# Reordered scorer, first exponents and last batch in a fused gating, mixture and masked-pooling kernel

## The chip, the cores and the metric

One core of a Trainium2 chip. The metric is the device time of one execution in microseconds (us); lower is better. The output is [8, 512, 256] in float32.

## The reference

Eight batches of 512 tokens with 256 features. Two layers add to x.

```
u  = zX * lap_x(x) + zY * lap_y(x) + zR * x * (1 - x)
w  = softmax over the top 2 of (u @ router)             # 8 experts
x  = x + sum_e w_e * (act(u @ gate_up_e + b_e) @ down_e + b'_e)
score = tanh(x @ W1 + b1) @ v                           # per token
mask(j, l) = l <= j | l >= j | l != j                   # by the batch's kind 0, 1, 2
pooled = softmax_l(score, masked) @ x / count(mask row)
x  = x + fp8(pooled / s_in) @ fp8(kernel / s_k) * (s_in * s_k) + bias
```

The fp8 rounding is done with float32 operations on a grid; everything else is float32, with products in two or three parts (hi and lo) where a plain one would lose digits.

## The kernel before, in words

The engines run programs of their own, in strict program order, and meet at semaphores. SP issues the loads and stores, GpSimd (POOL) the indirect and the accumulating transfers. PE is TensorE, ACT ScalarE, DVE VectorE. There are four stages: the differences and the routing (to about 130 us), 71 blocks of 128 gathered rows through their expert (to about 348 us), mixing and scoring (to 403 us), and the pooling with the fp8 layer. The change touches the last two.

**Mixing and scoring**, n = 0 to 7. DVE adds the two weighted expert rows of batch n to X (`mix_of`, semaphore `mixed`), and makes X_lo of the batch before (`x_low`, once X_hi is there). ACT's `scores_of(n)` copies X_hi(n), then the two halves of the transposed batch from PSUM (xT), then does the tanh of the batch before (`hide(n-1)`). PE does `x_transposed(n)`, `hide(n-1)` (the scorer's product with W1) and `score(n-2)` (the product with v), then at the end hide(7), score(6), score(7). hide(n) waits for both xT(n), score(n) for tanh(n).

**Statistics.** The 4096 scores stand in score_col [128, 32]; PE transposes them, and DVE makes running maxima over each row from the left and from the right, from them the row maxima for the three kinds of mask (`row_max`), the maximum of each row (own_max, spread by a product), `gap` and `reach`. ACT copies or exponentiates them in parts: decay, four diagonals of decay_lhs, reach_lhs, max_rhs, in that order. Four low parts follow on DVE, and then POOL multiplies max_rhs with the spread matrix once for each batch, `spread_gaps(n)`, all eight in a row. PE's `exponents(n)` begins with the product of score_lhs and gaps_rhs(n).

**Pooling**, a software pipeline over n = 0 to 9. PE: sums_of(n), feed_forward(n-2), pool_of(n), quant_transposed(n-1), exponents(n+2). ACT: exponents(n+1), ffn_out(n-2), pool_out(n) (pooled, then scaled), turned_quant(n-1). DVE: rounding(n-1) (two operations on grid, lift, quant), norms(n), lows(n+1) (probs_lo, falls, states), add_bias(n-2). POOL: `add_up(n)` waits for ffn_sum(n) and for the store of X(n), and adds ffn_sum to the output in memory with an accumulating transfer. ffn_sum has two buffers: add_bias(n) waits until add_up(n-2) has landed. SP stores X(n) as soon as batch n is mixed.

Of the kernel before, what the change touches and what calls it, by code (L numbers as in the profile page):

```python
# [25 lines left out]
ALU = mybir.AluOpType  # L26
ACT = mybir.ActivationFunctionType
# [53 lines left out]
def adaln_ffn_kernel(nc, x, zx, zy, zr, kinds, router_w, gate_up_w, gate_up_b, down_w, down_b,  # L81
# [7 lines left out]
    TB = S // P  # L89
    NT = B * TB  # L90
# [22 lines left out]
    with ExitStack() as ctx:  # L113
        def sem(name):
            return ctx.enter_context(nc.semaphore(name))
# [127 lines left out]
        from_left = sb("from_left", [P, P])  # L243
        from_right = sb("from_right", [P, P])
# [118 lines left out]
        hi_set = sem("hi_set")  # L363
# [28 lines left out]
        begun = [sem(f"begun{i}") for i in range(B)]  # L392
# [29 lines left out]
        def _(sp):  # L422
# [54 lines left out]
            for n in range(B):  # L477
                sp.wait_ge(mixed, n + 1)
                sp.dma_start(out_v[n], X[:, n * TB:(n + 1) * TB, 0:H]).then_inc(begun[n], 16)

        @block.gpsimd
        def _(pool):
# [101 lines left out]
            def add_up(n):  # L584
                pool.wait_ge(ffn_sum_ready, n + 1)
                pool.wait_ge(begun[n], 16)
                pool.dma_start(out_v[n], ffn_sum[:, n % 2], accum_op=ALU.add).then_inc(result_stored[n % 2], 16)  # L587

            pool.wait_ge(lo_set, 4)
            for n in range(B):  # L590
                spread_gaps(n)
            for n in range(B):
                add_up(n)
            for s in range(2):
                pool.wait_ge(result_stored[s], 16 * (B // 2))

        @block.scalar
        def _(a):
# [127 lines left out]
            a.activation(score_lhs[0:2 * R], bank[0][0:2 * R, 0:P], ACT.Copy).then_inc(hi_set, 1)  # L726
            a.wait_ge(gap_col_ready, 1)
            a.activation(decay[:], gap[:], ACT.Exp).then_inc(hi_set, 1)
            for q in range(QS):
                op = a.activation(diagonal(q), gap[:], ACT.Exp)  # L730
            op.then_inc(hi_set, 1)
            a.wait_ge(reach_ready, 1)
            a.activation(reach_lhs[0:2 * R], reach[0:2 * R].unsqueeze(1).broadcast_to([2 * R, QS, R]),
                         ACT.Copy).then_inc(hi_set, 1)
            a.wait_ge(max_ready, 1)
            a.activation(max_rhs[2 * R:P], row_max[2 * R:P], ACT.Copy).then_inc(hi_set, 1)
# [38 lines left out]

            exponents(0)
            for n in range(B + 2):
                if n + 1 < B:
                    exponents(n + 1)
                if n >= 2:  # L780
                    ffn_out(n - 2)
                if n < B:
                    pool_out(n)
                if 1 <= n <= B:
                    turned_quant(n - 1)

        @block.tensor
        def _(pe):
# [174 lines left out]
            def exponents(n, kind):  # L963
                pe.wait_ge(spread_ready, n + 1)
                wait_count(pe, probs_ready, n)
                pe.matmul(bank[0][:], score_lhs[:], gaps_rhs[:, n].rearrange("p t n -> p (t n)"), start=True, stop=False)
                pe.matmul(bank[0][:].rearrange("p (t n) -> p t n", n=P), ident_b[:],
                          masks[:, ds(kind), :].broadcast_to([P, TB, P]), start=False, stop=True).then_inc(gaps_psum, 1)
                wait_count(pe, fall_ready, n)
                pe.matmul(bank[1][:], reach_lhs[:].rearrange("p q r -> p (q r)"),  # L970
                          gaps_rhs[:, n].rearrange("p t n -> p (t n)"), start=True, stop=True).then_inc(falls_psum, 1)
                wait_count(pe, states_lo_ready, n)
                for t in range(TB):
# [57 lines left out]
            pe.wait_ge(lo_set, 4)  # L1031
            pe.wait_ge(tables, DECAY_CLEAR)
            exponents(0, kind_of(0))
            exponents(1, kind_of(1))
            for n in range(B + 2):
                if n < B:
                    sums_of(n)
                if n >= 2:
                    feed_forward(n - 2)
                if n < B:  # L1040
                    pool_of(n)
                if 1 <= n <= B:
                    quant_transposed(n - 1)
                if n + 2 < B:
                    exponents(n + 2, kind_of(n + 2))

        @block.vector
        def _(dve):
# [309 lines left out]
            dve.memset(max_rhs[0:R * 2].bitcast(F32), 1.0)  # L1358
            def x_low(n):
# [12 lines left out]
            def stat(instruction):  # L1372
# [5 lines left out]
            LOWEST = -3.0e38  # L1378
            dve.tensor_tensor_scan(from_left[:], score_row[:], score_row[:], LOWEST, ALU.max, ALU.max)
            stat(dve.tensor_tensor_scan(from_right[:, ::-1], score_row[:, ::-1], score_row[:, ::-1], LOWEST,  # L1380
                                        ALU.max, ALU.max))
            dve.tensor_scalar(own_max[:], ident[:, 0:R], from_left[:, P - 1:P], None, ALU.mult).then_inc(own_max_ready, 1)
            dve.tensor_tensor(around[:, 1:P - 1], from_left[:, 0:P - 2], from_right[:, 2:P], ALU.max)
            dve.tensor_copy(around[:, 0:1], from_right[:, 1:2])
            dve.tensor_copy(around[:, P - 1:P], from_left[:, P - 2:P - 1])
            stat(dve.tensor_scalar(row_max[:], from_left[:], kind_col[:, PREFIX:PREFIX + 1], None, ALU.add))
            stat(dve.scalar_tensor_tensor(out=row_max[:], in0=from_right[:], scalar=kind_col[:, POSTFIX:POSTFIX + 1],
# [4 lines left out]
            dve.tensor_tensor(gap[:], score_col[:, 0], max_bank, ALU.subtract).then_inc(gap_col_ready, 1)  # L1392
# [4 lines left out]
            dve.wait_ge(hi_set, 5)  # L1397
            dve.wait_ge(max_ready, 1)
            dve.tensor_tensor(score_lhs[R:2 * R], score_row[R:2 * R], score_lhs[R:2 * R].bitcast(F32),
                              ALU.subtract).then_inc(lo_set, 1)  # L1400
            dve.tensor_tensor(reach_lhs[R:2 * R], reach[R:2 * R].unsqueeze(1).broadcast_to([R, QS, R]),
                              reach_lhs[R:2 * R].bitcast(F32), ALU.subtract).then_inc(lo_set, 1)
            dve.tensor_tensor(max_rhs[3 * R:P], row_max[3 * R:P], max_rhs[3 * R:P].bitcast(F32),
                              ALU.subtract).then_inc(lo_set, 1)
# [47 lines left out]

            lows(0)
            for n in range(B + 2):
                if 1 <= n <= B:
                    rounding(n - 1)
                if n < B:
                    norms(n)
                if n + 1 < B:
                    lows(n + 1)  # L1460
                if n >= 2:
                    add_bias(n - 2)

# [22 lines left out]
```

## Time and profile before

| what | us |
|---|---|
| median of 3 runs | 501.81 (499.57 to 503.17) |
| the profiled execution | 498.88 |
| its span, first to last instruction | 496.9 |
| busy in the span: PE, DVE, POOL, ACT | 380.9, 368.8, 252.0, 221.3 |
| mean granted TensorE clock | 0.855 |

The profile is of one execution. Its span is shorter than its time by what lies around it. Busy time is a sum over the span; which engine sets the pace differs from stage to stage and is read from stretches of the trace. PEclk is the granted clock of TensorE as a share of full speed.

### The profile page before, as it was taken

Reading aid. Unit: us, or ns where it says so; the run is one execution under the profiler, and the core shown is the slowest. Engines: PE = TensorE matmul, PEld = TensorE weight load, DVE = VectorE, ACT = ScalarE, POOL = GpSimd, SP = SyncE. Lnnn points to the kernel's source line nnn. Section 1 sums busy time; section 2 is a strip of 40 time slices with the busy share of each in tenths; the row PEclk is TensorE's granted clock in tenths of the full one; section 3 lists DMA queues with packets and bytes.
Section 4 is the critical chain, followed back from the end, with each engine's and each line's share of the span. In section 5 each row is a group of like instructions: output and inputs, shape, how many; then the busy total and the mean of one; then the engine's idle time right before and its main releaser. Section 6 shows DMA issues by size and latency. Waiting matters only on the chain.

```text
span 496.9 us, 7816 instructions
## 1 busy us (share of the span) xinstructions
PE 380.9 (77%) x2269; PEld 325.7 (66%) x2269; DVE 368.8 (74%) x877; ACT 221.3 (45%) x480; POOL 252.0 (51%) x236
## 2 busy tenths in 40 slices
PE   0768886514299999999999999998188949887740
PEld 0657775513188888888888888887144538786630
DVE  7897777599667777888878877785499553778740
ACT  3473433100034444444444544443165545799850
POOL 6997564036557677777766666753300051021221
PEclk9976669655589999999999999999579966899975
DMA  6465651100033222322322322230699200034444
GB/s 215 142 212 174 191 174 48 39 0 1 21 95 97 86 87 77 106 87 91 94 90 83 97 86 69 92 86 26 206 350 368 92 0 1 1 54 76 63 71 78
DMA packets 39544, 50.02 MB, mean 101 GB/s; under 512 B 6126, under 2 KB 33138, under 8 KB 39506
## 3 DMA queue, kind: packets, MB, share of 16 engines
q0 software_dynamic: 11040, 21.90, 17.3%
q1 hardware_dynamic: 24242, 23.43, 14.9%
q10 hardware_dynamic: 4224, 4.19, 2.6%
q8 instruction: 22, 0.36, 0.3%
q14 instruction: 16, 0.13, 0.1%
HBM read 28.49 MB, written 21.89 MB: 101 GB/s over the span
## 4 chain that ended last, share of the span: by engine, by line
PE 55%; DVE 18%; issue 12%; POOL 6%; ACT 4%; DMA 2%; SPq 1%; DVEq 0%; POOLq 0%; ACTq 0%
PE bank L865 30%; PE bank L862 5%; PE bank L826 4%; PE bank L856 3%; PE bank L881 3%; DVE lift L1441 2%; DVE flow L1192 2%; ACT scaled L761 2%; DVE pair L1188 2%; POOL x_lo L515 2%; POOL pair L518 2%; DVE flow L1097 2%; PE bank L1000 2%; DVE gu_lo L1101 2%; PE bank L805 1%
## 5 line engine op out<-in xcount | busy, mean ns | idle before, releaser
L567 POOL DMA_INDIRECT y_rows<-outs,slot_dst x71 | 71.9, 1013 | 50.5 <-issue 29.9
L547 POOL DMA_INDIRECT rows<-u_rows,slot_src x71 | 71.8, 1012 | 24.8 <-issue 19.8
L672 ACT ACTIVATE tanh<-gate 128x256 f32<-128x256 f32 x71 | 29.6, 417 | 99.8 <-DVE gate L1240 99.8
L865 PE MATMUL bank<-gu_hi,rowT_lo 128*128 x142 | 57.1, 402 | 0.0
L865 PE MATMUL bank<-gu_hi,rowT_hi 128*128 x142 | 56.6, 399 | 0.0
L865 PE MATMUL bank<-gu_lo,rowT_hi 128*128 x142 | 56.4, 397 | 0.0
L1240 DVE TENSOR_SCALAR gate<-bank 128x256 f32<-128x256 f32 x71 | 30.2, 425 | 23.9 <-PE bank L865 23.7
L657 ACT ACTIVATE rowT_hi<-bank 128x256 fp32r<-128x256 f32 x71 | 27.0, 380 | 40.0 <-PE bank L856 40.0
L587 POOL DMA_DIRECT2D out<-ffn_sum x8 | 12.2, 1528 | 63.4 <-DVE ffn_sum L1450 63.4
L1258 DVE TENSOR_TENSOR actT_lo<-bank,actT_hi 128x256 fp32r<-128x256 f32 x71 | 30.1, 425 | 15.5 <-ACT actT_hi L677 15.1
L865 PE MATMUL bank<-dn_lo,actT_hi 128*128 x142 | 40.2, 283 | 0.0
L865 PE MATMUL bank<-dn_hi,actT_hi 128*128 x142 | 40.0, 282 | 0.0
L865 PE MATMUL bank<-dn_hi,actT_lo 128*128 x142 | 39.9, 281 | 0.0
L826 PE MATMUL bank<-router_sb,uT 128*128 128x8 f32 x128 | 23.2, 318 | 16.2 <-DVE logits L1110 14.7
L826 PEld LDWEIGHTS bank<-router_sb,uT 128*128 128x128 f32 x128 | 22.5, 273 | 18.2 <-DVE logits L1110 16.1
L862 PE MATMUL bank<-gu_bias,ones 128*128 x71 | 34.3, 482 | 0.0
L580 POOL TENSOR_TENSOR gaps_rhs<-max_rhs,spread 128x512 fp32r<-128x512 f32 x8 | 8.9, 1147 | 48.0 <-DVE decay_lhs L1405 48.0
L1224 DVE TENSOR_TENSOR rowT_lo<-bank,rowT_hi 128x256 fp32r<-128x256 f32 x71 | 29.5, 415 | 4.6 <-ACT rowT_hi L657 4.6
L677 ACT ACTIVATE actT_hi<-bank 128x256 fp32r<-128x256 f32 x71 | 27.5, 387 | 11.2 <-PE bank L881 11.2
L856 PE MATMUL bank<-ident,rows 128*128 128x128 f32 x142 | 27.9, 279 | 5.8 <-DMA rows<-u_rows,slot_src 5.8
L1245 DVE TENSOR_TENSOR glu<-gate,up 128x256 f32<-128x256 f32 x71 | 30.4, 428 | 2.4
L865 PEld LDWEIGHTS bank<-gu_lo,rowT_hi 128*128 128x128 f32 x142 | 27.0, 190 | 6.6
(267 smaller groups left out, 1139.9 us busy)
## 6 DMA issues: line engine op xcount, KB each, us to landing
picks<-y_rows SPq DMA_DIRECT2D x16, 512.0 KB, 8.0
X<-in_x SPq DMA_DIRECT2D x8, 512.0 KB, 5.4
raw_gu<-in_L_ffn_gate_up_proj SPq DMA_DIRECT2D x8, 512.0 KB, 4.1
u_rows<-flow ACTq DMA_DIRECT2D x8, 512.0 KB, 2.9
out<-X SPq DMA_DIRECT2D x8, 512.0 KB, 7.6
out<-ffn_sum POOLq DMA_DIRECT2D x8, 512.0 KB, 5.8
raw_dn<-in_L_ffn_down_proj SPq DMA_DIRECT2D x8, 256.0 KB, 4.9
rows<-u_rows,slot_src POOLq DMA_INDIRECT x71, 2.8
```

The source lines that it names most:

```text
L547: pool.indirect_dma_start(out=rows[:, s, :], out_offset=None, in_=u_rows, in_offset=bass.IndirectOffsetOnAxis(ap=slot_src[:, n:n + 1], axi ...
L567: pool.indirect_dma_start(out=y_rows, out_offset=bass.IndirectOffsetOnAxis(ap=slot_dst[:, m:m + 1], axis=0), in_=outs[:, m % UNROLL, :], i ...
L672: a.activation(tanh[:, s % 2], gate[:, s % 2], ACT.Tanh, scale=ALPHA).then_inc(tanh_ready, 1)
L677: a.activation(actT_hi[:, s % 2], bank[4 + s % 2][:, 0:KI * P].rearrange("p (k n) -> p k n", k=KI), ACT.Copy).then_inc(actT_hi_ready, 1)
L826: mm = pe.matmul(logit_bank[:, t, :], uT[:, half, t * P:(t + 1) * P], router_sb[:, half, :], start=(half == 0), stop=(half == KH - 1))
L856: mm = pe.transpose(bank[2 + s % 2][:, half * P:(half + 1) * P], rows[:, s, half * P:(half + 1) * P], ident[:])
L862: pe.matmul(acc, ones2[:], bias, start=True, stop=False)
L865: mm = pe.matmul(acc, left[:, part, :], right[:, ds(expert), part, :].rearrange("p e f -> p (e f)"), start=False, stop=(part == parts - 1 ...
L1224: dve.tensor_tensor(rowT_lo[:, d], bank[2 + d][:, 0:KH * P].rearrange("p (k n) -> p k n", k=KH), rowT_hi[:, d].bitcast(F32), ALU.subtract) ...
L1240: dve.tensor_scalar(gate[:, d], bank[d][:, 0:I], LIMIT, 0.5, ALU.min, ALU.mult).then_inc(gate_ready, 1)
L1245: dve.tensor_tensor(glu[:, d], gate[:, d], up[:, d], ALU.mult).then_inc(glu_ready, 1)
L1258: dve.tensor_tensor(actT_lo[:, d], bank[4 + d][:, 0:KI * P].rearrange("p (k n) -> p k n", k=KI), actT_hi[:, d].bitcast(F32), ALU.subtract) ...
```

## The change

In the mixing, PE does hide(n-1), x_transposed(n), score(n-1), and ACT copies xT(n) before X_hi(n). In the statistics from_left and from_right get a border column, so that one operation makes `around`; gap is computed behind row_max; ACT copies max_rhs first, then reach_lhs, then decay and the diagonals; DVE makes the low parts one by one as they come and multiplies gaps_rhs of batch 0 itself; PE waits for each part where it uses it. POOL makes gaps_rhs of batches 1 to 7, each behind a probs_lo two batches back, then the accumulating stores of batches 0 to 6. Batch 7 is done in halves of 256 tokens from scaled to the output: DVE adds ffn_sum to X in SBUF, and SP stores each half plainly. The pipeline's loops end one batch earlier, and norms(7) comes before rounding(6).

```
@@ SP
-            for n in range(B):
+            for n in range(LAST_B):
                 sp.wait_ge(mixed, n + 1)
-                sp.dma_start(out_v[n], X[:, n * TB:(n + 1) * TB, 0:H]).then_inc(begun[n], 16)
+                sp.dma_start(out_v[n], X[:, n * TB:(n + 1) * TB, 0:H]).then_inc(begun, 16)
+
+            for h in range(2):
+                own = slice(h * HALF, (h + 1) * HALF)
+                sp.wait_ge(half_result, h + 1)
+                sp.dma_start(out_v[LAST_B][:, own], X[:, LAST_B * TB:(LAST_B + 1) * TB, 0:H][:, own]).then_inc(half_stored, 16)
+            sp.wait_ge(half_stored, 32)
@@ POOL
             def add_up(n):
                 pool.wait_ge(ffn_sum_ready, n + 1)
-                pool.wait_ge(begun[n], 16)
+                pool.wait_ge(begun, 16 * LAST_B)
                 pool.dma_start(out_v[n], ffn_sum[:, n % 2], accum_op=ALU.add).then_inc(result_stored[n % 2], 16)
-            pool.wait_ge(lo_set, 4)
-            for n in range(B):
+            pool.wait_ge(first_spread, 1)
+            for n in range(1, B):
+                wait_count(pool, probs_lo_ready, n - 1)
                 spread_gaps(n)
-            for n in range(B):
+            for n in range(LAST_B):
                 add_up(n)
@@ ACT
             def scores_of(n):
                 s = n % 2
                 a.wait_ge(mixed, n + 1)
-                a.activation(X_hi[:, n * TB:(n + 1) * TB, 0:H], X[:, n * TB:(n + 1) * TB, 0:H],
-                             ACT.Copy).then_inc(X_hi_ready, 1)
                 for half in range(KH):
                     a.wait_ge(xT_psum, 2 * n + half + 1)
                     wait_count(a, hidden_psum, n - 1)
                     a.activation(xT[:, s, half], bank[2 * s + half][:], ACT.Copy).then_inc(xT_ready, 1)
+                a.activation(X_hi[:, n * TB:(n + 1) * TB, 0:H], X[:, n * TB:(n + 1) * TB, 0:H],
+                             ACT.Copy).then_inc(X_hi_ready, 1)
                 if n >= 1:
                     hide(n - 1)
...
+            def pool_out_halves():
+                a.wait_ge(norm_ready, LAST_B + 1)
+                a.wait_ge(lifted, LAST_B)
+                for h in range(2):
+                    own = slice(h * HALF, (h + 1) * HALF)
+                    for j in range(h * HALF, (h + 1) * HALF):
+                        a.wait_ge(pool_psum, TB * LAST_B + j + 1)
+                        a.activation(pooled[:, j, :], bank[4 - j % 2][:, 0:H], ACT.Copy,
+                                     scale=norm[:, LAST_B % 2, j:j + 1]).then_inc(pooled_ready, 1)
+                    a.wait_ge(pooled_ready, TB * LAST_B + (h + 1) * HALF)
+                    a.activation(scaled[:, own], pooled[:, own], ACT.Copy, scale=scales[:, 3:4]).then_inc(half_scaled, 1)
...
             exponents(0)
-            for n in range(B + 2):
...
+            for n in range(LAST_B):
+                exponents(n + 1)
                 if n >= 2:
                     ffn_out(n - 2)
...
+                pool_out(n)
+                if n >= 1:
                     turned_quant(n - 1)
+            ffn_out(LAST_B - 2)
+            pool_out_halves()
+            turned_quant(LAST_B - 1)
+            ffn_out(LAST_B - 1)
+            a.wait_ge(ffn_sum_ready, LAST_B - 1)
+            for h in range(2):
+                half_out(h)
@@ PE
             for n in range(B):
+                if n >= 1:
+                    hide(n - 1)
                 x_transposed(n)
                 if n >= 1:
-                    hide(n - 1)
-                if n >= 2:
-                    score(n - 2)
+                    score(n - 1)
             hide(B - 1)
-            score(B - 2)
             score(B - 1)
...
-                pe.wait_ge(spread_ready, n + 1)
+                if n == 0:
+                    pe.wait_ge(lo_set, 2)
+                    pe.wait_ge(first_spread, 1)
+                else:
+                    pe.wait_ge(spread_ready, n)
@@ DVE
+            dve.tensor_tensor(around[:], from_left[:, 0:P], from_right[:, 2:P + 2], ALU.max)
...
             dve.tensor_scalar(row_max[:], row_max[:], reach_max[:, 0:1], -1.0, ALU.max, ALU.mult).then_inc(max_ready, 1)
-            dve.wait_ge(hi_set, 5)
-            dve.wait_ge(max_ready, 1)
+            dve.tensor_tensor(gap[:], score_col[:, 0], max_bank, ALU.subtract).then_inc(gap_col_ready, 1)
+            dve.wait_ge(score_hi_set, 1)
...
+            dve.wait_ge(lo_set, 2)
+            dve.tensor_tensor(gaps_rhs[:, 0], max_rhs[:].bitcast(F32).unsqueeze(1).broadcast_to([P, TB, P]),
+                              spread[:, 0, 0:TB].bitcast(F32).unsqueeze(2).broadcast_to([P, TB, P]),
+                              ALU.mult).then_inc(first_spread, 1)
...
             lows(0)
-            for n in range(B + 2):
-                if 1 <= n <= B:
+            for n in range(LAST_B):
+                if n >= 1:
                     rounding(n - 1)
...
+                norms(n)
+                lows(n + 1)
                 if n >= 2:
                     add_bias(n - 2)
+            norms(LAST_B)
+            rounding(LAST_B - 1)
+            add_bias(LAST_B - 2)
+            for h in range(2):
+                rounding_half(h)
+            add_bias(LAST_B - 1)
+            for h in range(2):
+                result_half(h)
```

LAST_B is 7 and HALF is 2 (tiles of 128 tokens). `half_out(h)` copies the turned quarter out of PSUM and, behind PE's half product, the scaled result; `rounding_half` and `result_half` are the four rounding operations, and the bias and the sum with X, on 512 columns.

## Rows read from the trace of the kernel before

**Rows 1.** Busy time by stretch: the mixing; PEclk, DMA share and GB/s at the end.

```profile
355.80:391.00 35.20, 27.26 (x129) 16.27 (x130) 34.76 (x75) 20.07 (x29) 0.00 (x0) 0.85 0.97 318
```

**Rows 2.** Timeline of one batch in the mixing: start, length, instruction, idle before.

```profile
380.72 1.06 ACT L701 ACTIVATE X_hi<-X 128x1024 fp32r<-128x1024 f32 x1 [0.67 <-DVE X L1346]
...
380.83 1.06 PE L924 MATMUL bank<-ident,X 128*128 128x128 f32 x8 [0.53 <-DVE X L1346]
381.69 1.06 ACT L706 ACTIVATE xT<-bank 128x512 f32<-128x512 f32 x2
381.73 3.38 DVE L1346 SCALAR_TENSOR_TENSOR X<-picks,tok_w,X 128x256 f32<-128x256 f32 x8
...
381.82 1.93 PE L933 MATMUL bank<-xT,w_sb 128*64 128x512 f32 x4
...
383.68 1.05 PE L940 MATMUL bank<-v_sb,hidden 64*128 64x1 f32 x8
383.79 0.68 ACT L714 ACTIVATE hidden<-bank,b_sb 64x512 f32<-64x512 f32 x1 [1.04 <-PE bank L933]
...
385.26 1.06 PE L924 MATMUL bank<-ident,X 128*128 128x128 f32 x8 [0.53 <-DVE X L1346]
```

**Rows 3.** Timeline, the first batch of the mixing.

```profile
359.33 1.94 PE L924 MATMUL bank<-ident,X 128*128 128x128 f32 x8 [10.47 <-DVE X L1346]
...
361.31 0.60 ACT L706 ACTIVATE xT<-bank 128x512 f32<-128x512 f32 x1 [0.26 <-PE bank L924]
```

**Rows 4.** Timeline, the end of the scores.

```profile
395.38 1.94 PE L940 MATMUL bank<-v_sb,hidden 64*128 64x1 f32 x16
...
397.36 0.28 ACT L721 ACTIVATE score_col<-bank 128x128 f32<-128x128 f32 x1 [1.19 <-PE bank L940]
```

**Rows 5.** Busy time by stretch: a hole of TensorE in the pooling and after it.

```profile
421.40:423.90 2.50, 0.01 (x1) 0.04 (x1) 2.29 (x4) 0.62 (x2) 0.00 (x0) 1.00 0.00 0
424.30:427.60 3.30, 3.30 (x20) 3.03 (x18) 1.50 (x3) 2.05 (x5) 0.00 (x0) 0.50 0.01 2
```

**Rows 6.** Timeline, the end of the statistics.

```profile
401.25 0.29 DVE L1396 TENSOR_SCALAR row_max<-row_max,reach_max 128x128 f32<-128x128 f32 x1
...
403.33 1.04 POOL L580 TENSOR_TENSOR gaps_rhs<-max_rhs,spread 128x512 fp32r<-128x512 f32 x1 [48.04 <-DVE decay_lhs L1405]
```

**Rows 7.** Timeline, the first low parts of the pooling.

```profile
406.82 1.08 DVE L1412 TENSOR_TENSOR probs_lo<-probs,probs_hi 128x512 fp32r<-128x512 f32 x1 [3.58 <-ACT probs L744]
...
407.99 1.35 DVE L1416 TENSOR_TENSOR falls<-fall,falls 32x512 fp32r<-32x512 f32 x1
```

**Rows 8.** Timeline of VectorE, batch 4 to 5, and two DMA issue rows.

```profile
448.96 0.69 DVE L1412 TENSOR_TENSOR probs_lo<-probs,probs_hi 128x512 fp32r<-128x512 f32 x1
...
450.85 0.69 DVE L1450 TENSOR_TENSOR ffn_sum<-ffn,bias_f 128x1024 bf16<-128x1024 bf16 x1
...
452.61 0.69 DVE L1435 TENSOR_SCALAR grid<-scaled 128x1024 int32<-128x1024 int32 x1 [1.06 <-ACT scaled L761]
...
u_rows<-flow ACTq DMA_DIRECT2D x8, 512.0 KB, 2.9
...
out<-ffn_sum POOLq DMA_DIRECT2D x8, 512.0 KB, 5.8
```

**Rows 9.** Timeline of the last two batches, and the stretch of the last moving data.

```profile
468.73 0.69 DVE L1435 TENSOR_SCALAR grid<-scaled 128x1024 int32<-128x1024 int32 x1 [1.06 <-ACT scaled L761]
...
468.88 0.25 PE L990 MATMUL bank<-states,falls 128*128 128x2 f32 x1
...
472.71 0.18 DVE L1425 RECIPROCAL share<-bank 128x4 f32<-128x4 f32 x1
...
479.51 1.23 DVE L1444 TENSOR_TENSOR quant<-lift,grid 128x1024 bf16<-128x1024 f32 x1
...
486.58 1.28 POOL L587 DMA_DIRECT2D out<-ffn_sum  x1 [3.66 <-DVE ffn_sum L1450]
...
491.00:492.00 1.00, 0.00 (x0) 0.00 (x0) 0.00 (x0) 0.00 (x0) 0.00 (x0) 0.50 0.54 100
```

More of the change, by code:

```diff
@@ L391, in adaln_ffn_kernel @@
         ffn_sum_ready = sem("ffn_sum_ready")
-        begun = [sem(f"begun{i}") for i in range(B)]
+        half_scaled = sem("half_scaled")
+        half_round = sem("half_round")
+        half_quant = sem("half_quant")
+        half_turned = sem("half_turned")
+        half_quantT = sem("half_quantT")
+        half_ffn = sem("half_ffn")
+        half_ffn_out = sem("half_ffn_out")
+        half_sum = sem("half_sum")
+        half_result = sem("half_result")
+        half_stored = sem("half_stored")
+        begun = sem("begun")
         result_stored = [sem(f"result_stored{i}") for i in range(2)]
@@ L725, in _ @@
             a.wait_ge(tables, DECAY_CLEAR)
-            a.activation(score_lhs[0:2 * R], bank[0][0:2 * R, 0:P], ACT.Copy).then_inc(hi_set, 1)
+            a.activation(score_lhs[0:2 * R], bank[0][0:2 * R, 0:P], ACT.Copy).then_inc(score_hi_set, 1)
+            a.wait_ge(max_ready, 1)
+            a.activation(max_rhs[2 * R:P], row_max[2 * R:P], ACT.Copy).then_inc(max_hi_set, 1)
+            a.wait_ge(reach_ready, 1)
+            a.activation(reach_lhs[0:2 * R], reach[0:2 * R].unsqueeze(1).broadcast_to([2 * R, QS, R]),
+                         ACT.Copy).then_inc(reach_hi_set, 1)
             a.wait_ge(gap_col_ready, 1)
-            a.activation(decay[:], gap[:], ACT.Exp).then_inc(hi_set, 1)
+            a.activation(decay[:], gap[:], ACT.Exp).then_inc(decay_hi_set, 1)
             for q in range(QS):
                 op = a.activation(diagonal(q), gap[:], ACT.Exp)
[L731 to L736, printed above, removed]
+            op.then_inc(decay_hi_set, 1)
             def exponents(n):
@@ L1030, in _, with half_fed @@
             pe.wait_ge(ends_set, 2)
-            pe.wait_ge(lo_set, 4)
             pe.wait_ge(tables, DECAY_CLEAR)
+            def half_fed(h):
+                pe.wait_ge(half_quant, h + 1)
+                if h == 0:
+                    pe.wait_ge(quantT_ready, LAST_B)
+                qT = bank[5 - 5 * h][:].bitcast(BF16)
+                for half in range(KH):
+                    for i in range(HALF):
+                        mm = pe.transpose(qT[:, (half * HALF + i) * P:(half * HALF + i + 1) * P],
+                                          quant[:, LAST_B % 2, h * HALF + i, half * P:(half + 1) * P], ident_b[:])
+                mm.then_inc(half_turned, 1)
+                pe.wait_ge(half_quantT, h + 1)
+                pe.wait_ge(ffn_ready, 2 * LAST_B)
+                for i in range(HALF):
+                    t = h * HALF + i
+                    for half in range(KH):
+                        mm = pe.matmul(bank[6 + h][:, i * F:(i + 1) * F],
+                                       quantT[:, half, t * P:(t + 1) * P], k_quant[:, half, :],
+                                       start=(half == 0), stop=(half == KH - 1))
+                mm.then_inc(half_ffn, 1)
             exponents(0, kind_of(0))
             exponents(1, kind_of(1))
-            for n in range(B + 2):
-                if n < B:
-                    sums_of(n)
+            for n in range(B):
+                sums_of(n)
                 if n >= 2:
                     feed_forward(n - 2)
-                if n < B:
-                    pool_of(n)
-                if 1 <= n <= B:
+                pool_of(n)
+                if n >= 1:
                     quant_transposed(n - 1)
@@ L1451, in add_bias, with rounding_half @@
                                   ALU.add).then_inc(ffn_sum_ready, 1)
+            def rounding_half(h):
+                own, s = slice(h * HALF, (h + 1) * HALF), LAST_B % 2
+                dve.wait_ge(half_scaled, h + 1)
+                if h == 0:
+                    dve.wait_ge(quantT_psum, LAST_B - 1)
+                dve.tensor_scalar(grid[:, s, own].bitcast(I32), scaled[:, own].bitcast(I32), EXPONENT_BITS, None,
+                                  ALU.bitwise_and).then_inc(half_round, 1)
+                dve.wait_ge(half_round, 3 * h + 1)
+                dve.tensor_scalar(grid[:, s, own], grid[:, s, own], FP8_LEAST_NORMAL, FP8_GRID, ALU.max,
+                                  ALU.mult).then_inc(half_round, 1)
+                dve.wait_ge(half_round, 3 * h + 2)
+                dve.tensor_tensor(lift[:, own], scaled[:, own], grid[:, s, own], ALU.add).then_inc(half_round, 1)
+                dve.wait_ge(half_round, 3 * h + 3)
+                dve.tensor_tensor(quant[:, s, own], lift[:, own], grid[:, s, own], ALU.subtract).then_inc(half_quant, 1)
@@ new lines, in result_half @@
+            def result_half(h):
+                own, s = slice(h * HALF, (h + 1) * HALF), LAST_B % 2
+                dve.wait_ge(half_ffn_out, h + 1)
+                if h == 0:
+                    dve.wait_ge(result_stored[s], 16 * (LAST_B // 2))
+                dve.tensor_tensor(ffn_sum[:, s, own], ffn[:, s, own], bias_f[:].unsqueeze(1).broadcast_to([P, HALF, F]),
+                                  ALU.add).then_inc(half_sum, 1)
+                dve.wait_ge(half_sum, h + 1)
+                rows_of = X[:, LAST_B * TB + h * HALF:LAST_B * TB + (h + 1) * HALF, 0:H]
+                dve.tensor_tensor(rows_of, rows_of, ffn_sum[:, s, own], ALU.add).then_inc(half_result, 1)
@@ L1453, in _ @@
             lows(0)
-            for n in range(B + 2):
-                if 1 <= n <= B:
+            for n in range(LAST_B):
+                if n >= 1:
                     rounding(n - 1)
[L1457 to L1460, printed above, removed]
+                norms(n)
+                lows(n + 1)
                 if n >= 2:
                     add_bias(n - 2)
+            norms(LAST_B)
+            rounding(LAST_B - 1)
+            add_bias(LAST_B - 2)
@@ L1466 @@
+            for h in range(2):
+                rounding_half(h)
+            add_bias(LAST_B - 1)
+            for h in range(2):
+                result_half(h)
 _INS = ["x", "condB_zX", "condB_zY", "condB_zR", "itok_B_0_2", "L0_ffn_router_weight", "L0_ffn_gate_up_proj",
```

62 lines of the change are left out of this document (42 added, 20 removed).

## The prediction, made before the changed kernel was run

> **What bounds the kernel now.** I read the busy time by stage first. In the mixing VectorE is busy 34.76 of 35.20 us [rows 1]: this stage is VectorE's, and every other engine has room. The timeline of one batch there tells in what order the others serve it [rows 2]. X_transposes (PE L924) start when a batch is mixed, at 380.83 and next at 385.26, so the period is 4.43 us: 3.38 of VectorE for the mix and the rest for X_lo. ScalarE does X_hi (380.72), the two xT copies (from 381.69, 1.06 together) and the tanh (383.79). TensorE does transposes, the scorer product (381.82) and the score (383.68) of an earlier batch, and then waits for the mix. The chain of waits goes through this stage as VectorE's work, then through the statistics (398 to 403), and then from batch to batch of the pooling through scaled, grid, lift, quant, share and the first product, 8.06 us each (rounding begins at 452.61 and, two batches on, at 468.73 [rows 8, 9]), ending in one store of POOL.
>
> **Scorer products and xT moved: the mixing.** The new orders have to be laid beside each other. TensorE: hide(n-1), transposes(n), score(n-1), hide(n). ScalarE in its scores_of(n): xT(n) twice, X_hi(n), tanh(n-1). Score(n-1) needs tanh(n-1). Before, it was score(n-2), whose tanh lay a whole batch back; now the tanh stands behind copies that wait for transposes(n). So a loop closes: transposes(n), xT(n), X_hi(n), tanh(n-1), score(n-1), hide(n), transposes(n+1). hide(n) has its xT early, but stands behind score(n-1).
>
> Its length at the full clock, from the start T of the transposes: the second xT copy follows the end of the transposes by 0.04 us (359.33 + 1.94 against 361.31 [rows 3]), so with 1.06 of transposes [rows 2] it begins at about T + 1.15, where the first copy, some 0.65 behind T, lets it (one copy costs 0.5 in a row of two). X_hi begins at T + 1.64. From X_hi to the operation behind it are 0.97 (380.72 to 381.69): tanh at T + 2.61, 0.68 long, and 0.05 to TensorE: score at T + 3.34. A score costs 0.95 (16 products in 1.94 [rows 4]), so hide begins at T + 4.29. From hide to the work behind it are 1.86 (381.82 to 383.68): the next transposes start at T + 6.15. That is 1.7 more than VectorE's 4.43, so TensorE and ScalarE, by turns, become the bound and VectorE waits. X_hi behind xT costs nothing itself: X_lo(n) comes after the next mix.
>
> The clock decides how much more. In each turn TensorE now has from T + 1.06 to T + 4.29 only the score's 0.95. In the pooling's first batches a stretch of 2.5 us with 0.01 us of matmuls was followed by 3.3 us at the lower of the two levels (1.2 of 2.4 GHz), fully at work [rows 5]. At that level the transposes take 1.94 in place of 1.06 [rows 3], hide some 3.6 for 1.86, and the score, whose low-clock price no row shows, between 0.95 and 1.9. So a turn costs 6.15 at the full clock and 6.15 + 0.9 + 1.75 + 0.9 = 9.7 at the lower. I take hide, which comes right behind the hole, and half of a score as slow, and the transposes as fast again: 6.15 + 1.7 + 0.4 = 8.25. The nearest row for it is that stretch of 3.3 us behind a hole.
>
> The first turn: transposes(0) stay at 359.33, xT(0) ends at 361.91, hide(0) is slow (3.6), so T_1 = 365.5. T_7 = 365.5 + 6 x 8.25 = 415.0, where before it was 380.83 + 2 x 4.43 = 389.69. From T_7 to score_col it was 7.67 (397.36 [rows 4]); now it is 4.29 + 1.86 + tanh 0.78 + score 1.05 = 7.98, with the same slow hide and half scores 10.1. **Scores ready at 425.1 instead of 397.36: +27.7 us**; at the full clock throughout 402.4 + 8.0: +13.0; at the low one 423.7 + 11: +37. What was meant to go, the two scores at the end in a row, is one less (0.95), and the loop takes more than that already in its first turn.
>
> **Statistics to the first exponents.** One operation for three on the edges of around saves 0.13. Row_max ends at 401.54 now [rows 6]; with gap behind it, some 0.25 earlier. Max_rhs is copied at once, in place of after decay, four diagonals and reach: copy 0.3, low part 0.3, then the product gaps_rhs(0) on VectorE, 0.69 by the quiet 128x512 subtraction [rows 8], against 1.04 on POOL. It ends near 402.7 against 404.37: -1.7. The reach and decay parts then run under the first matmuls. The first probs_lo took 1.08 beside POOL's gaps and falls 1.35 [rows 7], against 0.69 for the quiet one; gaps(1) is over by then, gaps(2) still meets falls. That gives 0.4 more: **-2.1**, from -1 (VectorE's product as slow as probs_lo beside POOL, nothing at falls) to -3.
>
> **Gaps spaced on POOL.** The gaps themselves have time, each waiting for a probs_lo two batches ahead of its use. But POOL is one queue, and all of them stand ahead of add_up(0). Gaps(7) now waits for the sixth probs_lo, which VectorE makes at 448.96 to 449.65 [rows 8]. POOL is through at about 450.8, where add_up(0) stood at 435.72 before. And add_bias(2), at 450.85 on VectorE, waits for that store to land, as it uses the same half of ffn_sum; behind it in VectorE's queue stand rounding(4) and all that follows. A store's landing has a median of 5.8 us from issue [rows 8]; the last one moved data until 4.9 us after its start [rows 9]. Landed at 456.3, bias 0.7: rounding(4) begins at 457.1 instead of 452.61, and that is on the loop of the batches: **+4.5**, between +2 and +7 by a quicker or slower landing. Batch 5 finds add_up(1) landed; it happens once.
>
> **The last batch.** Norms(7) comes ahead of rounding(6): its last sum ends at 469.1 [rows 9], so rounding(6) starts 0.7 later, and its four operations (3.98, from 468.73 to share at 472.71) end at 473.4; but pooled(7) may now start once lift(6) is done, near 472.2, rather than behind share and its product. After the bias of batch 5 (0.7) come the halves, 2.0 each by size: second half of quant done at 478.1, against 480.74. From there to the start of the store it was 5.84 [rows 9]. The halves shorten each link, but the second stands behind the first and behind batch 6, and X + ffn_sum (about 0.7) is new: I keep 5.8, so 483.9. Then SP stores 256 KB: I take 2.5 (512 KB have a median of 2.9 in the quickest row [rows 8]), landed at 486.4. Before, POOL started at 486.58 and data moved to 491.5. **-5.1**, between -3 and -6.5. The 5 us behind the last data stay.
>
> **Sum.** 27.7 - 2.1 + 4.5 - 5.1 = +25.0. The profiled execution took 498.88 (span 496.9 and 2.0 around it), so 523.9; it lies 2.9 below the median of the runs, so the median becomes 526.8. I say 527.
>
> **Rivals.** (a) The loop stays at the full clock: 13.0 - 2.7 = +10.3, 512. For it: the clock held 1.00 through the idle 2.5 us themselves [rows 5], and a turn holds 2.9 us of products. Against it: the 3.3 slow us behind them, and a hole here comes back every turn. The Trainium skill ("TensorE: Matmul & The Clock Gate", "What's actually happening") says that for modeling the ramp penalty is under 1% of a typical kernel's span, which speaks for this rival: the loop would cost little above its full-clock length. The trace so far speaks against it, with a hole followed by slow work [rows 5]. My slow parts add 15 us to the sum. (b) The loop at the low clock throughout: 37 - 2.7 = +34, 536. (c) Not slower: the loop doesn't close, because TensorE takes hide(n) and the next transposes before a score that waits. Mixing then stays at 4.43, and all is 0 - 2.1 + 4.5 - 5.1 = -2.7, 499. It decides where the turn falls below 4.43. Against it: in the timeline TensorE keeps the written order, transposes, scorer, score, and idles 0.53 us before the next transposes [rows 2]. The Trainium skill (same page, "What happens when you issue a matmul") says that only weight loads are pulled ahead and that the matmuls stay in program order. (d) No stall of POOL's, the store landing before VectorE comes to it: 4.5 less, 522, inside the range.
>
> **How the numbers follow.** Forecast with (d) 0.70, between 517 and 533; (a) 0.12, 508 to 516; (b) 0.14, 532 to 539; (c) 0.04. Range 512 to 535. A measurement here tells about 1% from no change. Faster 0.01, same 0.03, slower 0.96.
>
> **What would show it.** Transposes of two batches 6 to 9.7 us apart in the mixing, TensorE idle between transposes and score with tanh as releaser, VectorE below 80% busy there; the granted clock of that stage under 0.85; score_col near 425. First gaps on VectorE. The start of the first accumulating store behind the last gaps_rhs, and a wait of some 5 us at ffn_sum L1450. The end from share(7) shorter by some 5. I am wrong if the period stays at 4.4, and wrong by 15 us if the clock stays up.

## The result, and the profile after

The changed kernel took 527.62 us (median of 4 runs, 523.74 to 529.69), the kernel before 500.69 (4 runs on the same chip, 494.11 to 503.17). The ratio is **1.061** (95%: 1.045 to 1.077): slower. Every ratio here is taken from the runs within 1.5% of their kernel's fastest, the medians from all runs, so a ratio isn't their quotient (here 1.054). The two profiled executions have spans of 527.9 and 496.9, +31.0; the difference of the medians is 26.9.

I cut both spans at the same instructions: the start of the first transposes, the copy into score_col, and `share`, VectorE's reciprocal in norms(n), once for each batch of the pooling. Share(0) stands at 447.26 now and at 414.33 before.

```
us of the profiled execution            before   after   change
span's start to first transposes        359.33  364.12    +4.8
first transposes to score_col            38.03   69.70   +31.7
score_col to share(0)                    16.97   13.44    -3.5
share(0) to share(4)                     34.20   33.02    -1.2
share(4) to share(6)                     16.12   22.76    +6.6
share(6) to the end of the span          32.25   24.86    -7.4
```

The first line is unchanged code; 4.8 is less than the runs of one kernel differ among themselves, and I put it down to no edit. The rest adds up to +26.2.

**The mixing.** First the stretch's busy time (stretch, its length; then busy us and instruction count of PE, PEld, DVE, ACT, POOL; granted clock; DMA share, GB/s):

```profile
364.00:434.00 70.00, 52.42 (x160) 27.19 (x160) 32.99 (x69) 21.50 (x33) 0.00 (x0) 0.67 0.43 142
```

VectorE does the same work in 33 us as before, but has 70 for it. In [rows 1] it was the full engine; now no engine is, and the granted clock is 0.67. A stage in which nothing is full is set by waits. The view of waits has (waiting instruction, releaser: us in all, times, longest):

```profile
ACT xT L727 <- issue: 35.2, 6, 6.5
DVE X_lo L1442 <- ACT X_hi L728: 29.0, 7, 6.7
...
ACT xT L727 <- PE bank L975: 16.8, 6, 12.3
PE bank L991 <- ACT hidden L737: 16.6, 8, 2.3
```

TensorE's score (L991) waits for the tanh, and ScalarE's xT (L727) for the transposes; in the 35.2 us under "issue", for which the view finds no releaser, ScalarE stands ahead of xT while TensorE does score and hide. VectorE's wait for X_hi is where it has its idle time; it is no link of the loop.

The timeline of two turns (start, length, instruction, idle before; weight loads left out) has the loop in order, to be laid beside [rows 2]:

```profile
396.33 1.97 PE L975 MATMUL bank<-ident,X 128*128 128x128 f32 x8
...
398.34 0.60 ACT L727 ACTIVATE xT<-bank 128x512 f32<-128x512 f32 x1 [0.21 <-PE bank L975]
...
398.83 1.05 ACT L728 ACTIVATE X_hi<-X 128x1024 fp32r<-128x1024 f32 x1
...
399.78 0.67 ACT L737 ACTIVATE hidden<-bank,b_sb 64x512 f32<-64x512 f32 x1
...
400.50 1.05 PE L991 MATMUL bank<-v_sb,hidden 64*128 64x1 f32 x8 [2.20 <-ACT hidden L737]
...
401.48 3.47 PE L984 MATMUL bank<-xT,w_sb 128*64 128x512 f32 x4
...
404.88 1.20 PE L975 MATMUL bank<-ident,X 128*128 128x128 f32 x8
...
407.64 0.67 ACT L737 ACTIVATE hidden<-bank,b_sb 64x512 f32<-64x512 f32 x1
...
408.37 1.72 PE L991 MATMUL bank<-v_sb,hidden 64*128 64x1 f32 x8 [2.29 <-ACT hidden L737]
...
410.02 3.68 PE L984 MATMUL bank<-xT,w_sb 128*64 128x512 f32 x4
...
413.63 1.93 PE L975 MATMUL bank<-ident,X 128*128 128x128 f32 x8
```

Transposes, xT, X_hi, tanh, score, hide, transposes: 8.55 and 8.75 us a turn, where it was 4.43. Each turn has a hole of 2.2 to 2.3 us ahead of the score, and the hide behind it takes 3.5 or 3.7 in place of 1.93 [rows 2] (3.35 to 3.68 over all the turns). Transposes are slow (1.93 to 1.97) in one turn and quick (1.20 here) in the next, and scores take 1.05 or 1.72. Score_col comes at 433.82.

**Statistics.**

```profile
437.96 0.31 ACT L751 ACTIVATE max_rhs<-row_max 64x128 fp32r<-64x128 f32 x1 [2.86 <-DVE row_max L1475]
...
438.68 0.69 DVE L1485 TENSOR_TENSOR gaps_rhs<-max_rhs,spread 128x512 fp32r<-128x512 f32 x1
...
441.90 0.69 DVE L1499 TENSOR_TENSOR probs_lo<-probs,probs_hi 128x512 fp32r<-128x512 f32 x1 [1.23 <-ACT probs L767]
...
443.07 1.18 DVE L1503 TENSOR_TENSOR falls<-fall,falls 32x512 fp32r<-32x512 f32 x1 [0.48 <-ACT fall L771]
...
444.76 0.39 PE L1033 MATMUL bank<-X_hi,decay_lhs 128*128 128x258 f32 x1 [1.21 <-DVE states L1506]
...
447.26 0.18 DVE L1512 RECIPROCAL share<-bank 128x4 f32<-128x4 f32 x1 [2.56 <-PE bank L1048]
```

and the last two in the kernel before:

```profile
409.86 0.58 PE L975 MATMUL bank<-X_hi,decay_lhs 128*128 128x258 f32 x1 [0.74 <-DVE states L1419]
...
414.33 0.18 DVE L1425 RECIPROCAL share<-bank 128x4 f32<-128x4 f32 x1 [4.53 <-PE bank L990]
```

From score_col to the end of the first gaps_rhs are 5.55 us, before 7.01 [rows 4, 6]. The two low parts take 0.69 and 1.18, before 1.08 and 1.35 [rows 7], but falls now waits 0.48 for ScalarE, so from the end of gaps_rhs to the X_hi product shown only 0.1 is gained (5.39 for 5.49). From that product to share(0) are 2.50 us, before 4.47.

**The stall of POOL.** Timeline of POOL, then of VectorE:

```profile
481.48 1.54 POOL L602 TENSOR_TENSOR gaps_rhs<-max_rhs,spread 128x512 fp32r<-128x512 f32 x1 [6.52 <-DVE probs_lo L1499]
482.96 2.78 POOL L609 DMA_DIRECT2D out<-ffn_sum  x2
```

```profile
480.28 0.18 DVE L1512 RECIPROCAL share<-bank 128x4 f32<-128x4 f32 x1
...
489.19 0.69 DVE L1537 TENSOR_TENSOR ffn_sum<-ffn,bias_f 128x1024 bf16<-128x1024 bf16 x1 [6.62 <-DMA out<-ffn_sum]
489.81 0.69 DVE L1522 TENSOR_SCALAR grid<-scaled 128x1024 int32<-128x1024 int32 x1
...
494.03 0.18 DVE L1512 RECIPROCAL share<-bank 128x4 f32<-128x4 f32 x1
```

The first accumulating store starts behind the last row of gaps, and VectorE waits 6.62 us at ffn_sum for its landing, with grid, and so the next batch, in its queue behind. Share(4) to share(5) are 13.75 us for 8.06, share(5) to share(6) 9.01.

**The end.**

```profile
507.56 0.18 DVE L1512 RECIPROCAL share<-bank 128x4 f32<-128x4 f32 x1 [1.50 <-PE bank L1048]
...
516.34 0.69 DVE L1553 TENSOR_TENSOR quant<-lift,grid 128x512 bf16<-128x512 f32 x1
...
519.86 2.25 SPq L500 DMA_DIRECT2D out<-X  x2
...
521.02 0.69 DVE L1564 TENSOR_TENSOR X<-X,ffn_sum 128x512 f32<-128x512 f32 x1
```

The second half of quant ends at 517.03, 13.99 us after share(6) (503.04); before, quant ended at 480.74 [rows 9], 16.09 after share(6) (464.65). From there the last X is ready in 4.7 us (521.71); before, 5.84 passed to the start of the store.

### The profile page after: what moved, and what is told of

Same layout as the page of the kernel before. It is cut to its first block and busy times, and to the rows that moved or that the text cites. A ratio compares the mean times of both kernels' runs of the same rounds, so it can differ in the third digit from the quotient of the medians.

```text
span 527.9 us, 7826 instructions
## 1 busy us (share of the span) xinstructions
PE 399.8 (76%) x2269; PEld 333.5 (63%) x2269; DVE 372.2 (71%) x885; ACT 220.6 (42%) x482; POOL 253.3 (48%) x234
## 5 line engine op out<-in xcount | busy, mean ns | idle before, releaser
L877 PE MATMUL bank<-router_sb,uT 128*128 128x8 f32 x128 | 22.8, 315 | 15.3 <-DVE logits L1188 13.8
L556 POOL TENSOR_TENSOR flow<-flow,tile_no 128x568 bf16<-128x568 bf16 x8 | 16.4, 2048 | 33.3 <-DVE flow L1263 33.3
```

What stands on the lines that cost most here:

```text
L877: mm = pe.matmul(logit_bank[:, t, :], uT[:, half, t * P:(t + 1) * P], router_sb[:, half, :], start=(half == 0), stop=(half == KH - 1))
```

## Experiments

Between chips the kernel before itself differs (500.7 in the runs above, 524 to 545 below). So a ratio is always to the kernel before on the same chip, and stage lengths are compared within traces. The kernels came in three groups: mix_before, pe_alone, tanh_first and hole_filled (before: 530.16, 13 runs); stores_between, last_whole, first_gap_pool and switched (540.22, 17 runs); gaps_unspaced and act_alone (530.33, 13 runs). The changed kernel itself was not run on these three chips. Where an expectation gives a time of the whole, it stands against the 500.7 above; divided by it, it can be laid beside a ratio. "Mixing" is the stage from the first transposes to score_col. Unless said, each edit starts from the changed kernel.

**mix_before**: both orders of the mixing as before, the rest as changed.

```diff
-  xT(n) twice; X_hi(n); tanh(n-1)                 # ScalarE, batch n
+  X_hi(n); xT(n) twice; tanh(n-1)
-  hide(n-1); x_transposed(n); score(n-1)          # TensorE, batch n
-  ... at the end: hide(7); score(7)
+  x_transposed(n); hide(n-1); score(n-2)
+  ... at the end: hide(7); score(6); score(7)
```

> The changed kernel with both orders of the mixing as before the change (X_hi ahead of xT, transposes, hide(n-1), score(n-2)). Theory (the loop of transposes, xT, X_hi, tanh, score, hide cost the mixing some 32 us): the distance of two batches' transposes is 4.43 us again, from the first transposes to score_col 38.0 us, and the whole is 527.6 - 31.7 = 496 us, which is 5 below the kernel before, by the statistics, the first pooling batches and the end (3.5 + 1.2 + 7.4), less the wait for the first accumulating store (6.6). Rival (the loss lies in the statistics, the pooling or the end, or in the stages ahead, which ran 4.8 us later in the profiled run): 520 or more.

Measured: 524.99, ratio 0.995 (0.990 to 1.000), where 496 is 0.991; first transposes to score_col 38.17 us; share(4) to (5) 14.05; share(6) to end 25.18. The mixing's loss is all in the two orders; what is left of the change, its stall among it, comes out within 1% of the kernel before.

**pe_alone**: of mix_before's edit only ScalarE's half, so that TensorE's new order stands alone.

```diff
-  xT(n) twice; X_hi(n); tanh(n-1)                 # ScalarE
+  X_hi(n); xT(n) twice; tanh(n-1)
```

> The changed kernel with ScalarE's order of before (X_hi ahead of xT); TensorE's order is the new one. Theory: the loop still closes, but without X_hi behind xT in it, since X_hi then runs beside the transposes. At the full clock a turn is 6.15 less about 0.9, 5.2 us; with hide at the low clock 6.9 to 7.5. The hole before the score shrinks by 0.9 and the clock may hold more often. From the first transposes to score_col 50 to 60 us, the whole 508 to 518. Rival (xT ahead of X_hi is what closes the loop): 4.43 a turn, the whole 496.

**act_alone**: the counterpart, xT ahead of X_hi with TensorE's old order.

```diff
-  hide(n-1); x_transposed(n); score(n-1)          # TensorE
+  x_transposed(n); hide(n-1); score(n-2)
```

> The changed kernel with TensorE's mixing order of before and only ScalarE's xT ahead of X_hi. Theory: no loop (score(n-2) has its tanh a batch back), turns of 4.43 us; hide(7) may start 0.2 us earlier, but stands behind hide(6) and score(5) as before, so from the first transposes to score_col 38.0 us, nothing gained; the whole as with both orders of before, 0.995. Rival (X_lo waits for the later X_hi, so VectorE loses some 0.5 us a batch): turns of 4.9, 4 us more.

Measured: pe_alone 547.18, 1.032 (1.025 to 1.040; 508 to 518 is 1.015 to 1.035), mixing 56.47, turns of 6.9. Act_alone 527.85, 0.994 (0.989 to 0.999), mixing 38.17. So TensorE's order alone costs 18.3 us of mixing, ScalarE's alone nothing, both together 31.5 (69.70 less 38.17): the 13.2 that X_hi's place adds exist only where the loop is closed. The timeline of pe_alone:

```profile
419.92 0.67 ACT L737 ACTIVATE hidden<-bank,b_sb 64x512 f32<-64x512 f32 x1
...
420.64 1.05 PE L991 MATMUL bank<-v_sb,hidden 64*128 64x1 f32 x8 [1.30 <-ACT hidden L737]
421.62 3.61 PE L984 MATMUL bank<-xT,w_sb 128*64 128x512 f32 x4
```

Even a hole of 1.30 us a turn is followed by a hide at the low clock.

**tanh_first**: TensorE keeps the new order; the loop is opened on ScalarE.

```diff
 def scores_of(n):
+    if n >= 1: hide(n - 1)                          # the tanh
     a.wait_ge(mixed, n + 1)
     ...                                             # xT(n) twice, X_hi(n)
-    if n >= 1: hide(n - 1)
```

> The changed kernel with one move: ScalarE does the tanh of batch n-1 before it waits for batch n to be mixed, instead of behind xT(n) and X_hi(n). TensorE's new order and xT ahead of X_hi stay. Theory: the loop is open. Score(n-1) finds its tanh ready, the transposes come every 4.43 us by VectorE, the clock of the mixing stays at 1.00 once risen, and behind the last hide stands one score instead of two. From the first transposes to score_col 36 us (38.0 less 1.9), the whole 527.6 - 33.6 = 494. Rival (TensorE's order costs by itself, hide ahead of the transposes delaying them): 5 us or more a turn, 500 and over.

Measured: 525.82, 0.986 (0.976 to 0.996); mixing 37.40. Timeline:

```profile
417.29 0.68 ACT L737 ACTIVATE hidden<-bank,b_sb 64x512 f32<-64x512 f32 x1 [1.20 <-PE bank L984]
417.78 1.06 PE L975 MATMUL bank<-ident,X 128*128 128x128 f32 x8 [0.53 <-DVE X L1424]
418.77 1.05 PE L991 MATMUL bank<-v_sb,hidden 64*128 64x1 f32 x8
419.75 1.93 PE L984 MATMUL bank<-xT,w_sb 128*64 128x512 f32 x4
...
422.21 0.96 PE L975 MATMUL bank<-ident,X 128*128 128x128 f32 x7 [0.52 <-DVE X L1424]
```

The tanh runs beside the wait for the mix, score follows the transposes at once, and TensorE waits for VectorE again, 0.53 as in [rows 2]. The period is 4.43 in the last three turns, the clock of the stage 0.91. The mixing is 0.8 shorter than in mix_before, where 1.9 had been expected. From the last transposes to score_col it does gain 1.9 (5.76 for 7.68); but its first turn, with the slow hide(0) ahead of the transposes, takes 6.24 for 3.84, and the last transposes come 1.15 later.

**hole_filled**: the closed loop stays, and its hole is filled with products that nobody reads.

```diff
 x_transposed(n)
 if n >= 1:
+    for _ in range(18):
+        pe.transpose(bank[7][:, P:2 * P], ident[:], ident[:])
     score(n - 1)
```

> The changed kernel with 18 more transposes of the identity, into a part of a PSUM bank that nobody reads, between the transposes of batch n and score(n-1). They are extra work that takes the hole's time and no more (18 x 0.12 = 2.1 us at the full clock, in a hole of 2.3). Theory (of a turn of 8.75 us 6.15 are the loop and 2.6 the low clock): the granted clock of the mixing goes from 0.67 to over 0.9, a turn is 6.2 to 6.6, score_col 17 us earlier, the whole 510 to 514. Rival (the low clock is not from the hole, or the turn's 8.75 is from something else): turns of 8.75 or, with the added work on the path, 10; the whole 527 to 540.

Measured: 542.73, 1.024 (1.014 to 1.034; 510 to 514 is 1.019 to 1.027); mixing 51.94, turns of 6.22 to 6.41.

```profile
392.30:444.20 51.90, 48.10 (x286) 33.14 (x286) 32.91 (x69) 20.97 (x32) 0.00 (x0) 0.94 0.59 192
```

```profile
423.60 1.09 PE L975 MATMUL bank<-ident,X 128*128 128x128 f32 x8
424.53 2.13 PE L1006 MATMUL bank<-ident 128*128 128x128 f32 x18
426.26 0.67 ACT L737 ACTIVATE hidden<-bank,b_sb 64x512 f32<-64x512 f32 x1
...
426.99 1.05 PE L991 MATMUL bank<-v_sb,hidden 64*128 64x1 f32 x8 [0.33 <-ACT hidden L737]
427.96 1.93 PE L984 MATMUL bank<-xT,w_sb 128*64 128x512 f32 x4
429.83 1.09 PE L975 MATMUL bank<-ident,X 128*128 128x128 f32 x8
```

The most telling run: TensorE has 126 products more, and the stage is 17.8 us shorter than the changed kernel's. The clock is 0.94, every hide but the first is back at 1.93, and a turn is 6.2, the loop's own length; the added products end 0.33 ahead of the score, so they don't lengthen it. So of the 31.5 us that the orders cost, 13.8 (51.94 less 38.17) are the loop and 17.8 the clock. The Trainium skill ("TensorE: Matmul & The Clock Gate", "What's actually happening") has the ramp penalty, for modeling, under 1% of a typical kernel's span; here, with a hole in every turn, the low clock of this one stage is 3.4% of 527.9.

**switched**: as stores_between (below), but TensorE's start is drawn apart: transposes(1) go ahead of hide(0), and score(0) waits until batch 2, so that the slow hide(0) is off the first turn. ScalarE's first tanh stands behind X_hi(1).

```diff
- x_transposed(0)                                   # TensorE
- for n in 1..7: hide(n-1); x_transposed(n); score(n-1)
+ x_transposed(0); x_transposed(1); hide(0)
+ for n in 2..7: hide(n-1); x_transposed(n); [score(0) at n == 2]; score(n-1)
```

> stores_between with the first two batches of the mixing in the order of before (transposes(1), then hide(0)), and the new order from batch 2 on. With the tanh first alone the first turn was 6.24 us, as hide(0) at the low clock stood ahead of transposes(1), and T_7 came 1.3 us later than by VectorE alone. Theory: from the first transposes to score_col 36.2 us instead of 37.4, so about 1 us less than stores_between. Rival (VectorE had made it good, and X_lo behind X_hi sets it): 37.4, the same.

Measured: 531.96, 0.988 (0.981 to 0.994), mixing 39.50, 2.4 longer than in stores_between. The second and third turns took 7.12 and 6.46:

```profile
404.99 1.93 PE L988 MATMUL bank<-xT,w_sb 128*64 128x512 f32 x4 [0.77 <-ACT hidden L741]
...
409.75 3.63 PE L988 MATMUL bank<-xT,w_sb 128*64 128x512 f32 x4
```

A miss: hide(1) had to wait 0.77 us for a tanh, and hide(2) took 3.63. The slow first turn only moved.

**stores_between**: tanh_first, and POOL issues its stores between the gaps.

```diff
 for n in range(1, B):
     wait_count(pool, probs_lo_ready, n - 1)
     spread_gaps(n)
+    if n >= 5: add_up(n - 5)
-for n in range(LAST_B): add_up(n)
+for n in range(B - 5, LAST_B): add_up(n)
```

> The kernel with the tanh ahead of the wait for the mix, and on POOL add_up(n-5) directly behind the gaps of batch n for n = 5 to 7, in place of all gaps ahead of all stores. Theory (the wait at ffn_sum of batch 2 comes from POOL's order): share(4) to share(5) is 8.06 us instead of 13.5, share(5) to share(6) 8.06 instead of 9.0, so 6.4 us less than the kernel with the tanh first alone; against the kernel before 0.972 to 0.976. Rival (the wait is from the landing of the stores, or from the common count begun): 13.5 stays, 0.986.

Measured: 528.17 (521.06 to 531.08), **0.973** (0.964 to 0.982). VectorE at the same place as above:

```profile
486.66 0.18 DVE L1514 RECIPROCAL share<-bank 128x4 f32<-128x4 f32 x1
...
488.98 0.96 DVE L1539 TENSOR_TENSOR ffn_sum<-ffn,bias_f 128x1024 bf16<-128x1024 bf16 x1
...
494.84 0.18 DVE L1514 RECIPROCAL share<-bank 128x4 f32<-128x4 f32 x1
```

No wait at ffn_sum; share(4) to (6) 16.24, for 22.76. From the first transposes to the end of the span the stages add up to 126.5 us, 11.0 less than before the change (137.6). Its ratio is the lowest of all versions, below 1 and far below the changed kernel's 1.061.

**last_whole**: stores_between with the last batch in one piece, norms(7) behind rounding(6), and every X stored by SP as before.

```diff
-for n in range(B - 5, LAST_B): add_up(n)
+for n in range(B - 5, B): add_up(n)
-    sp.wait_ge(half_result, h + 1); ...            # SP's stores of X + ffn_sum
+    rounding(n - 1); norms(n); lows(n + 1); add_bias(n - 2)   # VectorE, n to B + 1
```

> The one above (stores_between) with the last batch whole again, as before the change: loops to the end, norms(7) behind rounding(6), one accumulating store of POOL. Theory (the halves with the plain store gain the 5 to 7.4 us of the end): from share(6) to the end of the span 32.2 us as before the change, against 24.9 in the changed kernel, so 6 to 7.4 us slower than stores_between. Rival (the end is set by the accumulating stores of batch 6 and the halves bring nothing): same as stores_between.

Measured: 536.73, 1.004 (0.997 to 1.011); share(6) to end 32.1, for 25.3 in stores_between. So the halves, with their plain stores and the earlier norms(7), are worth 6.8 us of the stage; no run parts the three. Between the two kernels' whole times, on one chip, lie 8.6 us by the medians and 3% by the ratios. That is more than the stage, and what the rest is stays open.

**first_gap_pool**: stores_between with gaps_rhs(0) on POOL again, max_rhs still copied first. One run.

```diff
-dve.tensor_tensor(gaps_rhs[:, 0], ...).then_inc(first_spread, 1)
-pool.wait_ge(first_spread, 1)
+pool.wait_ge(lo_set, 2)
+pool.tensor_tensor(gaps_rhs[:, 0], ...).then_inc(first_spread, 1)
```

> stores_between with the first gaps_rhs made on POOL instead of VectorE, at the same place. Theory: from max_rhs's low part to the first product of the exponents 0.4 us more (1.04 to 1.13 on POOL for 0.69), the rest of the start alike. Rival (POOL beside VectorE's small operations slows both, by 1 us and more).

Measured: score_col to share(0) 13.79, for 13.31: 0.5 from VectorE's product. A single run, 524.98, can't show a difference of this size in the whole.

**gaps_unspaced**: tanh_first without the wait for probs_lo on POOL; the stores stand behind all gaps, which are early now.

```diff
 for n in range(1, B):
-    wait_count(pool, probs_lo_ready, n - 1)
     spread_gaps(n)
```

> The kernel with the tanh first, and on POOL the gaps of batches 1 to 7 in a row without a wait between them, as before the change, then the stores. Theory (the stall of batch 4 is from gaps(7) waiting ahead of the stores, and the spacing earns little): share(4) to share(5) 8.06 us, all batches after the first 8.06, against 8.2 to 8.3 with the stores between; VectorE's first probs_lo and falls beside POOL take 1.1 and 1.35 in place of 0.69 and 1.2, 0.4 us later at share(0). The whole as stores_between within 1 us, 0.973 of the kernel before. Rival (the spacing is worth more, since VectorE's and POOL's work beside each other slows the first batches): 3 us and more slower than stores_between at share(1).

Measured: 520.76, 0.987 (0.975 to 0.998), for 0.973 expected. Score_col to share(0) 13.85, share(0) to (6) 50.70; stores_between has 13.31 and 50.84.

```profile
431.57 1.24 DVE L1498 TENSOR_TENSOR probs_lo<-probs,probs_hi 128x512 fp32r<-128x512 f32 x1 [1.23 <-ACT probs L766]
432.84 1.41 DVE L1502 TENSOR_TENSOR falls<-fall,falls 32x512 fp32r<-32x512 f32 x1
```

The low parts are slow again beside POOL (0.69 and 1.18 with spacing). From the first product of the exponents to the first X_hi product are 5.57 us here and 5.24 in stores_between, so they give 0.3 of the 0.5 that the spacing is worth. Its other side is the stall, which goes here as it does in stores_between. By stages these two kernels are equal within 1 us; their ratios come from different chips, so which is faster as a whole is not shown.

## Why the prediction was right

The forecast, 527 by +25.0, came out at 527.6. The medians differ by 26.9, as the kernel before came to 500.7 where I had 501.8; the spans differ by 31.0, of which 4.8 lie ahead of the changed stages. Against the terms stand the other 26.2. By its steps:

- **A loop closes, transposes to score to hide.** Right. Moving the tanh ahead (tanh_first) or taking back TensorE's order (act_alone) opens it; taking back only the place of X_hi (pe_alone) leaves it closed, and shorter. Rival (c) has fallen.
- **Its length at the full clock, 6.15.** Right: 6.22 or 6.23 in five of the seven turns of hole_filled.
- **The clock, 8.25 a turn.** The mechanism is right, and rival (a) has fallen by hole_filled. The term was small: the six turns took 51.93, 8.66 each. Hide took 3.35 to 3.68 in every turn, and transposes, which I had taken as fast, are slow in every second: 1.65 + 0.45 + 0.35 (half the score) over 6.22 is 8.67. Rival (b), the low clock throughout (9.7 a turn), overstated it.
- **Scores ready, +27.7.** Measured +31.7: 0.1 in the first turn (6.24 for 6.17), 2.4 in the six turns, and 11.53 for 10.1 behind T_7, where both scores and hide met the low clock.
- **Statistics, -2.1.** Measured -3.5 to share(0): 1.46 to the end of gaps_rhs (I had 1.7) and 0.1 from there to the X_hi product (I had 0.4 for the low parts). The rest, 2.0, I hadn't seen: TensorE's clock rose some 3 us after the pooling's first product, and 13 us after it before. Pe_alone prices it. Its statistics are the same, but its clock stayed at 0.50; from the X_hi product to share(0) it took 4.48 us and from score_col 15.28, where mix_before took 2.51 and 13.31. Why the clock rose sooner is open. The further 1.2 to share(4) I can't give to the edit: against the kernel before, that stretch is 0.6 shorter in tanh_first and 0.4 longer in stores_between.
- **Stall of POOL, +4.5.** The mechanism is right: stores_between removes it, and rival (d) has fallen. It measured 6.6, of which 5.7 from share(4) to share(5) (POOL's last product took 1.54, where I had about 1.1, and the store landed 6.2 us after its start, where I had 5.5) and 0.95 in the next, whose first products ran at the low clock after the idle time; I had priced no second batch.
- **Last batch, -5.1.** Right in kind, larger: -7.4 in the span, -6.8 by last_whole, which takes back all its parts together. Four links: quant's second half is 2.1 earlier behind share(6) (I had 2.6); X is ready 4.7 behind it, where I had kept the 5.84 to a store's start; from there to the last moved data (near 524.1) are 2.4, as taken (2.5, against 4.9 before); and the span ends 3.8 behind the last data, before 5.4. "I keep 5.8" and "the 5 us behind the last data stay" are the two terms that were off, by 1.1 and 1.6.

The terms were off by +4.0, -1.4, +2.1 and -2.3, and share(0) to (4) by -1.2. They cancel to +1.2, so the exact hit owes something to luck. That the change is slower, and by some 25 us, does not: that comes from the loop and its clock, +31.7 where I had +27.7.

## What to carry to other kernels

When a step is moved up a batch on one engine, write both engines' queues side by side and look for a path that leads from a batch's work back to the next batch's on the same engine. If there is one, its length replaces the busy engine's period, and orders that cost nothing alone (X_hi's place) lie on it. A loop that leaves TensorE a hole in each turn also costs clock behind it; fill the hole (1.061 became 1.024) or, better, open the loop, here by moving one tanh (0.986). And what is spaced out in an in-order queue holds back everything queued behind it, here the stores.

## Of the hardware, not expected

- Holes of 1.3 to 2.3 us in each turn kept the granted clock of a whole stage at 0.67 to 0.73; filled with idle products it was 0.94, and the longer program was quicker.
- Where a product of POOL (gaps_rhs, 128x512) and VectorE's falls overlapped, the one that started second took 0.5 us longer. In the trace after, POOL's took 1.04 from 442.67 and falls 1.18 from 443.07; later falls took 0.68 from 481.43 and POOL's 1.54 from 481.48. VectorE's probs_lo took 0.69 with POOL idle and 1.08 to 1.24 beside it.
- The unchanged stages ahead differ by chip: the first transposes start at 359 us in the trace before and at 387 to 402 in those of the experiments. In mix_before POOL's stores of the expert stage are 2.6 to 5.2 us apart by turns, where most were 2.89 apart before. Why is open; it is the reason to read only ratios on one chip.
